# Inside one step of a transformer layer's first half: z ahead of the denominators, variance ahead of the values, second scores and maxima ahead of the one-hot

## The reference, cut to what matters

```
h = top-k tokens of x by x.w + b, k = 204 of 256, in order of score, times sigmoid(score)
z = layernorm(h);  q, k, v = z Wq' + bq, z Wk' + bk, z Wv' + bv
h = h + (softmax(q k' / 8) v) Wo' + bo, rows with q[0] == 0 or k[0] == 0 masked out
u = layernorm(layernorm(h)) gamma + beta
logits = u Wr + br;  the two largest of 8 experts, mixed by their softmax
h = h + sum over the experts e of mix[e] (gelu(u W1[e] + b1[e]) W2[e] + b2[e])
```

## Time and profile before

| what | value |
|---|---|
| median of 3 runs | 264.24 us (263.4 to 267.89) |
| the profiled execution | 259.98 us, its span 257.8 us, granted TensorE clock 0.995 |
| TensorE matmuls busy | 225.0 us (87% of the span) |
| VectorE busy | 168.5 us (65%) |
| ScalarE busy | 139.7 us (54%) |
| GpSimd busy | 119.1 us (46%) |
| chain that ended last | TensorE 55%, VectorE 14%, issue 10%, DMA 9%, GpSimd 4%, SyncE queue 3%, ScalarE 3% |
| of it the experts' matmuls | L943 18%, L957 16% |

### The profile page before, as it was taken

One profiled execution on the slowest core, in us unless ns is written; L12 is line 12 of the kernel. 1 busy time (PEld: TensorE's weight loads), 2 busy tenths in 40 slices (PEclk: granted clock), 3 DMA queues, 4 the chain that ended last, 5 costly groups with the idle time before them and its releaser, 6 DMA issues.

```text
span 257.8 us, 5026 instructions
## 1 busy us (share of the span) xinstructions
PE 225.0 (87%) x1585; PEld 126.3 (49%) x1585; DVE 168.5 (65%) x512; ACT 139.7 (54%) x341; POOL 119.1 (46%) x112
## 2 busy tenths in 40 slices
PE   0579986979797999998989899999999999999991
PEld 0436764646465666676654254445344443443430
DVE  4996787887969787576574457284665638274353
ACT  1311384565656575747585536554566556457640
POOL 2515250434525252243123558458565636656652
PEclk9999999999999999999999999999999999999998
DMA  4156331223322320212444580672749376293911
GB/s 112 35 142 187 85 115 42 100 92 99 84 86 67 116 71 32 69 32 72 118 115 100 133 193 3 143 153 62 169 87 232 82 176 166 54 231 91 208 32 32
DMA packets 19795, 27.20 MB, mean 106 GB/s; under 512 B 5306, under 2 KB 16826, under 8 KB 19770
## 3 DMA queue, kind: packets, MB, share of 16 engines
q10 hardware_dynamic: 6256, 13.50, 22.3%
q1 hardware_dynamic: 13514, 13.38, 19.5%
HBM read 24.89 MB, written 1.98 MB: 104 GB/s over the span
## 4 chain that ended last, share of the span: by engine, by line
PE 55%; DVE 14%; issue 10%; DMA 9%; POOL 4%; SPq 3%; ACT 3%; DVEq 0%; POOLq 0%; ACTq 0%
PE PD L943 18%; PE PD L957 16%; DVE ahead L1127 4%; DMA rdbc<-rdend 3%; PE PD L869 3%; SPq L305 2%; PE PD L893 2%; DVE nmax L1171 2%; POOL rstd L447 2%; PE PD L903 2%; DMA srow<-scored 2%; PE PD L919 2%; ACT E L596 2%; PE PD L847 2%; PE PD L858 2%
## 5 line engine op out<-in xcount | busy, mean ns | idle before, releaser
L1280 DVE SCALAR_TENSOR_TENSOR ye<-PD,b_col,mb 128x408 f32<-128x408 f32 x64 | 40.8, 640 | 47.3 <-PE PD L957 46.5
L635 ACT ACTIVATE hid<-PD,b_eff 128x816 f32<-128x816 f32 x64 | 56.6, 935 | 27.3 <-PE PD L943 23.3
L471 POOL TENSOR_TENSOR acc<-acc,ye 128x408 f32<-128x408 f32 x52 | 54.7, 1052 | 32.2 <-DVE ye L1280 29.7
L943 PE MATMUL PD<-uT,w_g 64*128 64x408 f32 x256 | 53.1, 530 | 0.4 <-ACT hid L635 0.4
L957 PE MATMUL PD<-hid,w_sb 128*64 128x408 f32 x256 | 51.2, 519 | 0.2 <-DVE ye L1280 0.2
L596 ACT ACTIVATE E<-PD,nmax 102x204 f32<-102x204 f32 x64 | 26.5, 422 | 21.1 <-DVE nmax L1171 21.1
L943 PEld LDWEIGHTS PD<-uT,w_g 64*128 64x128 f32 x256 | 21.9, 186 | 19.2 <-ACT hid L635 6.1
L957 PEld LDWEIGHTS PD<-hid,w_sb 128*64 128x64 f32 x256 | 15.5, 136 | 32.0 <-issue 26.9
L447 POOL TENSOR_TENSOR rstd<-veps,neg_half 102x8 f32<-102x8 f32 x8 | 13.1, 1638 | 35.3 <-DVE veps L1144 35.3
L453 POOL TENSOR_TENSOR rstd<-veps,neg_half 102x8 f32<-102x8 f32 x8 | 13.1, 1639 | 29.8 <-DVE veps L1198 29.8
L1127 DVE SCALAR_TENSOR_TENSOR ahead<-srow,score,PD 128x256 bf16<-128x256 f32 x56 | 23.4, 474 | 1.8 <-DMA srow<-scored 1.8
(11 more groups left out here) (153 smaller groups left out, 332.4 us busy)
## 6 DMA issues: line engine op xcount, KB each, us to landing
mb<-mixd ACTq DMA_DIRECT2D x28, 408.0 KB, 5.7
srow<-scored SPq DMA_DIRECT2D x7, 512.0 KB, 3.9
rdbc<-rdend SPq DMA_DIRECT2D x16, 102.0 KB, 2.9
rbc<-rstd2d SPq DMA_DIRECT2D x16, 102.0 KB, 2.8
mb<-mixd SPq DMA_DIRECT2D x4, 408.0 KB, 5.2
X<-in_x ACTq DMA_DIRECT2D x6, 256.0 KB, 3.0
rbc<-rstdd SPq DMA_DIRECT2D x14, 102.0 KB, 2.8
out<-y SPq DMA_DIRECT2D x7, 204.0 KB
```

The source lines that it names most:

```text
L471: pool.tensor_tensor(acc[n % 4][:, :], H[:, n, :] if e == 0 else acc[n % 4][:, :], ye[k % 4][:, :], ALU.add)\
L635: act.activation(hid[k % 4][:, :, :], hid_ps[k % 2][:, :, 0:C], ACT.Gelu, bias=b1_eff[:, e:e + 1]).then_inc(hid_ok, 1)
L943: last = pe.matmul(hid_ps[k % 2][:, p, 0:C], w1_g[halves[p], e, :], uT[halves[p], n, :], start=True, stop=True)
L1280: dve.scalar_tensor_tensor(out=ye[k % 4][:, :], in0=y_ps[k % 2], scalar=b2_col[:, e:e + 1], in1=mb[n % MB][:, e, :], op0=ALU.add, op1=ALU. ...
```

## The change

Five places, in three of the engines' loops. VectorE (lines of the loop at the end of the vector function): `normalise(s - 1)` and `compare(u, 1)` come ahead of `one_over_den`; `var_eps(s)` ahead of `copy_v(s - 1)`; `row_max(s - 1, 1)` right behind `row_max(s - 1, 0)`, ahead of `normalise2` and `one_hot`. TensorE: `variance(s)` ahead of `values(u)`; `scores(u, 1)` right behind the first `attend`, ahead of `turn_std`, the second `attend`, `turn_den` and `centre2`. ScalarE: the exponentials of the second half come ahead of `copy_denT`, `copy_OT`, `gap_tanh`, `prepare_ffn` and `exp_neg`, with `squares2` between their two batches. Nothing is added or removed. The part behind the loop, with the last unit, and the programs of SyncE and GpSimd stay as they are.

```diff
@@ ScalarE
                 if (u := unit(s, 1)) is not None:
                     softmax(u, 0, [1])
+                    softmax(u, 1, [0])
+                if (u := unit(s, 3)) is not None:
+                    squares2(u)
+                if (u := unit(s, 1)) is not None:
+                    softmax(u, 1, [1])
                 if (u := unit(s, 2)) is not None:
                     copy_denT(u)
-                if (u := unit(s, 3)) is not None:
-                    squares2(u)
+                    copy_OT(u)
                 if s == UNITS - 1:
                     gap_tanh(0)
-                if (u := unit(s, 2)) is not None:
-                    copy_OT(u)
                 if s == 1:
                     prepare_ffn()
                 if s >= 1 and (u := unit(s, -2)) is not None:
                     exp_neg(u)
-                if (u := unit(s, 1)) is not None:
-                    softmax(u, 1)
@@ TensorE
                     project(u)
+                variance(s)
+                if (u := unit(s, 1)) is not None:
                     values(u)
-                variance(s)
...
                     attend(u, 0)
+                if (u := unit(s, 1)) is not None:
+                    scores(u, 1)
                 if s >= 1:
                     turn_std(s)
...
                     centre2(u)
-                if (u := unit(s, 1)) is not None:
-                    scores(u, 1)
@@ VectorE
-                if (u := unit(s, 2)) is not None:
-                    one_over_den(u)
                 normalise(s - 1)
                 if (u := unit(s, -1)) is not None:
                     compare(u, 1)
+                if (u := unit(s, 2)) is not None:
+                    one_over_den(u)
...
+                var_eps(s)
                 copy_v(s - 1)
-                var_eps(s)
...
                 row_max(s - 1, 0)
+                row_max(s - 1, 1)
...
-                row_max(s - 1, 1)
```

## The result

| | before | after |
|---|---|---|
| median | 263.82 us (4 runs, 261.05 to 267.89) | 275.64 us (4 runs, 272.53 to 280.44) |
| the profiled execution | 259.98 us, span 257.8, granted clock 0.995 | 273.79 us, span 271.4, granted clock 0.945 |

The ratio is 1.0391, with an interval of 1.0226 to 1.0555: the changed kernel is slower. (A ratio compares undisturbed runs only; the medians are over all runs.) The forecast was 272.0 us in a range of 264 to 276.

The account below looks back on a forecast made before the run. Before, VectorE's queue sets the seven z distances, with rbc 1.6 us early; after, z waits for rbc behind the denominators' write. Step changes sum to 7.8 us, taking the median from 264.24 to 272.0 us, range 264.0 to 276.0.

Parts of the forecast that it names:

- What decides: SyncE queue ahead of z: rbc stands behind the late denominators' write, issued 11.43 us after z, next z at 14.78.
- The offsets: Predicted start times within a step, counted from z, for the chain from second maximum to rbc and next z.
- The sum: Seven step changes, z0 to project behind z7: 1.2 + 1.1 + 0 + 0.5 + 1.5 + 2.5 + 1.0 = 7.8 us slower.
- z ahead of the denominators: VectorE: takes three small operations, 0.5 us or more, from z's path, if VectorE's queue stays what decides.
- The stall of rden_q and the port: VectorE: rden_q's stall (up to 0.92 us, median 0.17) may follow the denominators behind z, costing nothing in the sum.
- w_g: ScalarE, z0 to z1: w_g (1.1 us) loses its cover behind the second exponentials and delays the gate; step +1.2 us.
- The second scores: TensorE, VectorE: second maximum 2.3 us earlier (6.97), but uT (7.96), centre2 (8.68), squares2 (9.59) and rdenT (10.82) later.
- z could start near 13.0, a little under 14 in a step with a score sum: VectorE's own work behind var_eps2 (near 11.0) would allow this; the rbc wait to 14.78 hides it, cost 0.
- A: Rival, faster: VectorE's queue stays the bound, z rid of the denominators; 5.3 us gained, 258.9 us; chance 0.12.
- B: Rival, within 2%: rbc late, but uT and centre2 do not hold the exponentials; +4.0 us, 268.2 us; chance 0.26.
- C: Rival, slower still: the residual also waits for attn every step, +1 us in five steps, 277 us; chance 0.08.
- D: Rival: the expert half absorbs the moved order, so nothing changes, 264.5 us; chance 0.05.

Follow-up runs that it names:

- e1: Changed kernel with SyncE reading rbc ahead of the write of the denominators: 269.31 us, ratio 1.018 to before.
- e2: Changed kernel with copy_denT (rdenT) back ahead of the second half's exponentials, SyncE as it was: 268.29 us, ratio 1.016 to before.
- e10: Changed kernel with TensorE's holes filled by repeated matmuls, expert biases computed twice and TensorE's w_g part later in step 1: 274.37 us, ratio 1.056 to before.
- e6: Changed kernel with prepare_ffn (w_g) and exp_neg of step 1 back ahead of the second exponentials: 272.87 us, ratio 1.045 to before.
- e5: Changed kernel with normalise2 (uT) between the two row maxima on VectorE: 274.80 us, ratio 1.045 to before.
- e4: Kernel before with only z and the second comparisons moved ahead of the denominators: 257.23 us, ratio 0.978.
- e11: Kernel before with z ahead of the denominators and variance ahead of values, without the rest of the change: 258.79 us, ratio 0.984.
- e3: Kernel before with the change's ScalarE part alone: 283.72 us, ratio 1.084.
- e8: Kernel before with second scores and maxima moved up on TensorE and VectorE alone, ScalarE as before: 271.68 us, ratio 1.033.

## Why the prediction was right

**What decides.** Right as to what z waits for, and shown in three ways: rbc stands behind the denominators' write (chain and SyncE's timeline of after), and taking the one away from the other, by SyncE's order (e1) or by ScalarE's (e2), ends the waits and gives about half of the loss back. The six waits of z for rbc in after add up to 9.2 us; not all of that comes back, since other waits stand close behind. The offsets were, forecast and measured: second maximum 6.97 and 7.03, uT 7.96 and 8.02, centre2 8.68 and 8.74, squares2 9.59 and 9.70, rdenT 10.82 and 10.91, issue of rbc 11.43 and 11.53, z 14.78 and 14.79.

**The sum.** Distances, forecast and measured: z0 to z1 14.9 and 14.82, then 13.84 and 15.74, 14.25 and 14.10, 14.78 and 14.79, 14.78 and 15.12, 14.67 and 15.00, 15.2 and 15.58, project 0.72 and 1.29 behind z7. 7.8 us were forecast and 11.0 came. Behind project nothing was forecast and 2.6 us came. Of the missing 3.3 us ahead of project the largest piece, 1.9, is the step z1 to z2, at a granted clock of 0.85. e10 and e6 had 13.97 and 13.72 us there, at 1.00 and 0.91, close to the 13.84 of the forecast. The next, 0.57, stands between z7 and project: the second set of logits (TensorE, L919, from 132.71) takes 1.45 us at half clock, 0.81 before. The 0.33 of the step z5 to z6 is not the clock (1.00 there). The 2.6 us behind project also fall into a stretch at 0.74. So the term left out of the sum is TensorE's clock. I had taken matmul durations from rows at full level and never asked if they would stay there. By the medians the forecast of 7.8 us stands against 11.8. What the engine did before the fall at 37 us can be seen in the windows of after; the first line is the time around its start:

```profile
34.90:37.90 3.00, 1.25 (x11) 0.79 (x9) 2.88 (x4) 2.71 (x14) 0.00 (x0) 0.85 0.03 5
37.90:46.64 8.74, 7.93 (x43) 4.42 (x44) 6.75 (x30) 3.85 (x7) 1.04 (x1) 0.50 0.20 56
```

The same first stretch in e5:

```profile
34.90:37.90 3.00, 1.25 (x11) 0.79 (x9) 2.79 (x4) 2.62 (x14) 0.00 (x0) 1.00 0.02 4
```

In after TensorE was busy 1.25 of 3 us, waiting for exponentials and for the one-hot, and then had half the clock (the 1.2 GHz level) for 8.7 us, in which the sixteen select matmuls took 2.99 us in place of 1.60. That the new waits bring such falls about may be (the kernels with the change's early second scores lie at 0.945 to 0.974 in their profiled executions, e4 and e11 at 0.997 and 0.998), but it is not shown. e5 has the same instructions as after up to z3 and was as little busy in this stretch, and its clock stayed at 1.00 up to z1. e3, with the second scores in their old place, has clocks of 0.930 to 0.946 in its four executions, and the kernel before goes down to 0.956 itself.

**z ahead of the denominators.** Right in kind: "All of that leaves the path to z". It is worth 2.2% alone (e4: 257.23 us), more than I gave it in e4's expectation (259 to 261 us).

**The stall of rden_q and the port.** The prediction asked if it would follow the denominators to their new place. The traces say: it goes where a product of GpSimd is under way, `attn` (L460, 1.04 us) or the gated X (L441, 1.04 us, beside the rden_q of 0.70 us ahead of z5). Before, attn ran from 81.48 and rden_q from 81.62 to 82.54; in after attn ran from 60.69 and rden_qk from 60.99, for 0.76 us, but in the step of z3 attn was done by 74.68, rden_q began at 74.65, and took 0.17. In e8 attn starts at 85.20 and rden_qk takes 0.92 from 85.34. So both answers occur. The Trainium skill (SBUF — State Buffer, Who interferes with whom) says that such a pair shares a port and excludes each other; these rows agree. Behind z in the changed kernel the stall cost z nothing in the trace, as forecast.

**w_g.** The step z0 to z1 was right in size (14.9, measured 14.82), and the reason half right: the prediction got there by way of w_g, and e6 gives back 0.5 us only. Without w_g in the way VectorE's own queue is nearly as late, by its wait of 0.98 us ahead of the second maxima (e8 has that wait and no late w_g).

**The second scores.** Here the reasoning was too kind. It had how late uT, centre2 and squares2 would be to within 0.1 us, but used them only as a link to rdenT. e8 is 3.3% slower with rbc in time; net of the shorter waits for scores, some 3.2 of the 8.1 us in its profile are var_eps2 waiting for variance2. e1 and e2, which stay 1.8 and 1.6% over before, have this wait too (0.68 to 1.69 us in e1). That it is what keeps them there is not shown: 4.5 of e1's 8.5 us are one step at a clock of 0.70, and its step z5 to z6 is as short as before's in spite of the wait. The prediction also read VectorE as "otherwise busy" beside its two waits for scores; the trace of before has a third in each step, for the values (0.98 us in the step from z4). The prediction's "z could start near 13.0, a little under 14 in a step with a score sum" is that same bound: in after var_eps2 is at 11.18, and VectorE would have reached z at 87.10 - 0.67, which is 14.12 after z3. So in such a step of the changed kernel two late chains have nearly one length, 14.12 and 14.79 us, and with the longer one mended the other sets the distance.

**The rivals.** A (faster) would have needed rbc out by 9.5 us. When e1 and e2 gave it just that in the step from z3 (8.7, 8.9), z no longer waited for rbc, but the kernel was not faster, so A's price was wrong as well. B (uT and centre2 do not hold the exponentials): no, centre2 waits for uT (3.3 us in six waits) and squares2 for centre2. C (the residual waits for attn): no; between z0 and z7 of after it never waits for attn, only behind z7 (1.12 us). D: no, the experts absorbed nothing.

**Still open.** What makes the clock fall in one execution and not in the next, and so how much of the loss that is left in e1 and e2 is the clock and how much the late var_eps2; how much of the 2.6 us behind project it is; and why single executions of one kernel differ by 2 to 3% with little relation to their mean clock (after: 277.49 us at 0.973, 272.53 at 0.966).

## What to carry to other kernels

Before an instruction is moved, follow its result into the in-order queues behind it. Here a copy of 0.23 us, put behind four exponentials, held up a DMA that does not need it by 2 to 3 us a step from z2 on (from z3 to z4: rbc issued 11.53 us after z, 8.70 in e1). A wait that is moved ahead (the second maxima's) may come back one link later, so price everything that stands behind the moved instruction on its engine, up to the next wait; and when one mend gives half, look for a second chain of nearly the same length, and compare the granted clock step by step before you put a difference down to the order. Try each part of a reordering alone: here one part gains 2.2%, one nothing, and two lose.

## What the runs showed of the hardware that I had not expected

- Half clock on TensorE (0.50 granted) in stretches of up to 9 us inside a kernel that is otherwise at full level: sixteen select matmuls 2.99 us against 1.60, two centre matmuls 1.70 against 0.92. Ahead of 25 us the granted figure does not tell the speed: there sixteen select matmuls of before (from 22.16) take 2.99 us too, in windows whose figure is 1.00. With the same program up to z3 and the same 1.25 of 3 us busy just ahead of it, after had such a stretch ahead of z1 and e5 had not.
- A VectorE product of two 102 x 8 tiles in SBUF (rden_q or rden_qk) takes 0.17 us, or up to 1.05 us (e10) when it starts while GpSimd's attn or gated X is under way: it then ends within 0.04 us of the GpSimd operation, as in before (attn from 81.48 for 1.04 us, rden_q from 81.62 to 82.54). In a few places the operation is as long beside GpSimd's rstd (0.93 us from 146.71 in after), while in others beside rstd it takes 0.17; that is not explained.
